# The second norm's rows turned by a VectorE block transpose and a DRAM scratch, with several groups of instructions set elsewhere

## The reference

```
h = layernorm(x)
q, k, v = h @ wq.T + bq, h @ wk.T + bk, h @ wv.T + bv        # 32 heads of 32
scores  = einsum('bshd,bstd->bsht', q, k) / sqrt(32)         # heads against heads, within one row
context = einsum('bsht,bstd->bshd', softmax(scores), v)
x = x + context
h = layernorm(x)
top-2 of 8 experts by h @ gate_w.T, softmax over the two
x = x + h @ base_w.T + base_b + 2 * (LoRA, rank 16, of the chosen experts)
```

## Time and profile before

| | us |
|---|---|
| median of 3 runs | 1341.43 (1341.17 to 1341.87) |
| the profiled execution, its time | 1342.09 |
| its span, first to last instruction | 1339.8 |
| PE busy | 1276.6 (95%) |
| DVE busy | 1113.1 (83%) |
| ACT busy | 694.4 (52%) |
| POOL busy | 274.0 (20%) |

### The profile page before, as it was taken

How to read it: one execution, slowest core, us unless ns; L and a number is a source line. 1 busy time by engine, 2 the same in 40 slices (tenths; PEclk the granted TensorE clock), 3 DMA queues, 4 the chain that set the end, 5 groups by cost and what they waited for, 6 DMA issues and landing times.

```text
span 1339.8 us, 29902 instructions
## 1 busy us (share of the span) xinstructions
PE 1276.6 (95%) x12260; PEld 669.7 (50%) x12260; DVE 1113.1 (83%) x1590; ACT 694.4 (52%) x1080; POOL 274.0 (20%) x301
## 2 busy tenths in 40 slices
PE   4766999999999999999999999999999999999996
PEld 1433555555555555555555555545555555455543
DVE  5877888888888888888888888888888888888873
ACT  6775545444555454445555544455455444554540
POOL 0021212222112122222121222222222221121120
PEclk9988999999999999999999999999999999999998
DMA  9532221233322212322222222322212233222110
GB/s 363 220 95 46 84 75 50 63 78 78 78 59 66 66 60 63 78 78 67 66 70 58 60 71 78 78 63 67 74 52 57 78 79 78 63 64 73 36 33 32
DMA packets 162008, 103.68 MB, mean 77 GB/s; under 512 B 135616, under 2 KB 136640, under 8 KB 161984
## 3 DMA queue, kind: packets, MB, share of 16 engines
q1 hardware_dynamic: 161984, 103.36, 28.0%
HBM read 69.78 MB, written 16.78 MB: 65 GB/s over the span
## 4 chain that ended last, share of the span: by engine, by line
PE 90%; DVE 4%; ACT 3%; issue 2%; DMA 0%; SPq 0%; POOL 0%; DVEq 0%; ACTq 0%; POOLq 0%
PE acc L1235 24%; PE acc L1244 24%; PE dense_acc L1351 23%; PE attn_ps L1301 7%; PE dense_acc L1359 4%; PE attn_ps L1309 2%; PE low_ps L1334 1%; PE low_ps L1336 1%; PE low_ps L1335 1%; ACT work L357 1%; PE dense_acc L1374 1%; ACT base_parts L575 1%; DVE v_parts L842 1%; DVE base_parts L842 1%; ACT w_hi_q L599 0%
## 5 line engine op out<-in xcount | busy, mean ns | idle before, releaser
L1351 PE MATMUL dense_acc<-base_parts,x 128*128 128x512 f16 x1488 | 329.8, 379 | 0.0
L357 ACT COPY work<-work 32x512 f16<-32x512 f16 x384 | 236.0, 614 | 8.6
L1351 PEld LDWEIGHTS dense_acc<-base_parts,x 128*128 128x128 f16 x1488 | 143.1, 98 | 167.0
L935 DVE SCALAR_TENSOR_TENSOR work<-acc,acc_to_a,biases_sb 128x512 f32<-128x512 f32 x192 | 143.6, 749 | 51.0 <-PE acc L1244 45.7
L1235 PE MATMUL acc<-w_hi_k,x_hi 128*128 128x512 f16 x496 | 119.2, 384 | 6.0 <-DVE x_lo L966 6.0
L1235 PE MATMUL acc<-w_hi_q,x_hi 128*128 128x512 f16 x496 | 118.8, 383 | 0.0
L1244 PE MATMUL acc<-w_hi_q,x_lo 128*128 128x512 f16 x496 | 118.3, 382 | 0.0
L1244 PE MATMUL acc<-w_hi_k,x_lo 128*128 128x512 f16 x496 | 117.7, 380 | 0.0
L1244 PE MATMUL acc<-v_parts,x_lo 128*128 128x512 f16 x496 | 117.2, 379 | 0.0
L1235 PE MATMUL acc<-v_parts,x_hi 128*128 128x512 f16 x496 | 117.2, 379 | 0.0
L527 POOL TENSOR_TENSOR work<-work 128x1024 f16<-128x1024 f32 x31 | 66.0, 2130 | 231.0 <-ACT work L732 231.0
(11 more groups left out here) (194 smaller groups left out, 2136.2 us busy)
## 6 DMA issues: line engine op xcount, KB each, us to landing
work<-x_dram SPq DMA_DIRECT2D x64, 512.0 KB, 3.7
work<-work SPq DMA_DIRECT2D x256, 64.0 KB, 2.0
work<-x_dram SPq DMA_DIRECT2D x124, 128.0 KB, 3.7
out_dram<-work SPq DMA_DIRECT2D x31, 512.0 KB, 2.9
work<-wT_dram SPq DMA_DIRECT2D x17, 512.0 KB, 5.8
v_parts<-wT_dram SPq DMA_DIRECT2D x8, 512.0 KB, 13.7
base_parts<-wT_dram SPq DMA_DIRECT2D x5, 512.0 KB, 11.3
biases_sb<-bias_dram SPq DMA_DIRECT2D x4, 512.0 KB, 8.0
```

The source lines that it names most:

```text
L357: copy(diag[c * QD:(c + 1) * QD, :, c, j::NQ, :], src).then_inc(vdiag_ready, 1)
L935: nc.vector.scalar_tensor_tensor(out=ev[:, s], in0=acc[bank][:, :], scalar=acc_to_a[:, i:i + 1], in1=bias[g][:, s], op0=ALU.mult, op1=ALU. ...
L1351: nc.tensor.matmul(dense_acc[n][:, :], rows_part[:, k, :], w_part[:, k, cols], start=(k == 0 and m == 0), stop=False)
```

## The change

The rows of the second norm are no longer turned by PE, except those of the last tile. DVE transposes `xn` in blocks of 32 x 32 into `soft` (`turn_x2`, after `norm2`). ACT issues four DMAs (`park_x2`) that write it to a DRAM scratch in the order of a full transpose, in runs of 32 floats, and one DMA (`fetch_x2`) that reads it back into `soft`. `x2_high` and `x2_low` then read `soft` instead of PSUM. They stand later: `x2_high` after q's high part, `x2_low` after v1; the subtraction L1178 waits for `x2lo_ready`.

On PE `context(t-1)` moves into k's first half, ahead of the third of the eight `x_lo` matmuls; `experts(t-1)` moves behind the scores; `spread_stats` moves ahead of q's first half. On ACT `x1_high` moves from behind the first quarter of `spread_v` to behind `x2_high`, and `gate_exp` behind the exponential; on DVE `gate_top` moves behind L1178. v's loads share the semaphores of k's.

```diff
@@ scalar
+            def park_x2(p):
+
+                act.wait_ge(x2_turned, p + 1)
+                dst = turn_dram.rearrange("(b c) (k q t) -> q c k b t", b=NQ, k=KC, q=NQ)
+                for q in range(NQ):
+                    src = x2_flat[q * QD:(q + 1) * QD, :].rearrange("c (k b t) -> c k b t", k=KC, b=NQ)
+                    act.dma_start(dst[q], src).then_inc(x2_parked, 16)
+
+            def fetch_x2(p):
+
+                act.wait_ge(x2_parked, 16 * NQ * (p + 1))
+                act.dma_start(x2_flat, turn_dram).then_inc(x2_fetched, 16)
...
                 if nxt:
                     row_statistics(t + 1)
                     normalise_quads(t + 1)
+                park_x2(t - 1)
                 act.wait_ge(at_ready, t + 1)
...
                 nc.scalar.copy(k_parts[:, 0, :, :], turned3).then_inc(a_hi_ready, 1)
-                x2_high(t - 1)
+                fetch_x2(t - 1)
                 act.wait_ge(bt_ready, t + 1)
...
                 nc.scalar.copy(dense_parts[:, :, 0, :], turned3).then_inc(b_hi_ready, 1)
+                x2_high(t - 1)
+                if nxt:
+                    x1_high(t + 1)
...
+                act.wait_ge(shifted, t + 1)
+                nc.scalar.activation(soft, soft, ACT.Exp, scale=score_undo[:, 0:1]).then_inc(exped, 1)
                 if prev:
                     gate_exp(t - 1)
-                act.wait_ge(shifted, t + 1)
-                nc.scalar.activation(soft, soft, ACT.Exp, scale=score_undo[:, 0:1]).then_inc(exped, 1)
...
                 if nxt:
-                    x1_high(t + 1)
                     low_copy(t - 1)
@@ vector
+            def turn_x2(p):
+
+                dve.wait_ge(xn2_ready, p + 1)
+                dve.wait_ge(pt_ready, p + 1)
+                nc.vector.transpose(x2_flat, xn).then_inc(x2_turned, 1)
...
                     norm2(t - 1, x1)
+                    turn_x2(t - 1)
                     turn_first(t)
...
                 add_bias(t, 1, SECOND, 0, b_acc, b_biased)
-                x2_low(t - 1)
...
                 add_bias(t, 1, "v", 2, v_acc, v_biased)
+                x2_low(t - 1)
...
-                if prev:
-                    gate_top(t - 1)
                 dve.wait_ge(scored, t + 1)
+                dve.wait_ge(x2lo_ready, t)
...
                                         ALU.subtract).then_inc(shifted, 1)
+                gate_top(t - 1)
@@ tensor
                 for k in range(KC):
+                    if k == 2 and inside is not None:
+                        inside()
                     mm = nc.tensor.matmul(dst, x_lo[:, k, :], w_hi[g][:, k, cols], start=False, stop=(k == KC - 1))
...
-                project(FIRST, 0, 0, a_acc, any_low[0])
-                context(t - 1)
+                project(FIRST, 0, 0, a_acc, any_low[0], lambda: context(t - 1))
...
-                project(SECOND, 0, 2, b_acc, any_low[0])
                 if nxt:
                     spread_stats(t + 1)
+                project(SECOND, 0, 2, b_acc, any_low[0])
...
                 project(SECOND, 1, 0, b_acc, any_low[0])
-                turn2(t - 1)
...
                 project("v", 1, 2, v_acc, any_low[0])
-                experts(t - 1)
...
                 attend(scored)
+                experts(t - 1)
```

More of the change, by code:

```diff
@@ L228, in block_kernel @@
         low_ps = ps("low_ps", [P, HALF])
-        w_loaded = {g: [sem(f"w_{g}_loaded{k}") for k in range(KC)] for g in GROUPS}
+        w_loaded = {g: [sem(f"w_{g}_loaded{k}") for k in range(KC)] for g in ("k", "q", "base")}
+        w_loaded["v"] = w_loaded["k"]
+        loads = {"k": 1, "q": 1, "v": 2, "base": 1}
         ag_loaded = sem("ag_loaded")
@@ L343, in block_kernel @@
         base_free = sem("base_free")
+        x2_turned = sem("x2_turned")
+        x2_parked = sem("x2_parked")
+        x2_fetched = sem("x2_fetched")
+        turn_dram = nc.dram_tensor("turn_dram", (P, HID), F32, kind="Internal").ap()
         block = ctx.enter_context(nc.Block())
@@ L349, in block_kernel @@
         x1_last = soft
+        x2_flat = soft
+        x2_f32 = x2_flat.rearrange("p (k n) -> p k n", k=KC)
         C_ACT_FIRST, C_ACT_LAST, C_DVE = (0, 1), (2,), (3,)
@@ L581, in sums @@
                 for k in order[g][first:last]:
-                    act.wait_ge(w_loaded[g][k], 16)
+                    act.wait_ge(w_loaded[g][k], 16 * loads[g])
                     magnitude_sum(staged[g][k], w_chunk_sum[:, j, k:k + 1])
@@ L623, in x1_high @@
                     act.wait_ge(x1_turned_ready, t)
-                    act.wait_ge(scored, t)
+                    act.wait_ge(v_acc, 2 * t)
                     nc.scalar.copy(x_hi[:, :, :], x1_turned).then_inc(xhi_ready, 1)
@@ L631, in x2_high @@
                     act.wait_ge(w_lo_done["base"], place["base"][KC - 3] + 1)
-                act.wait_ge(turned2, p + 1)
-                nc.scalar.copy(x2_hi, rows_ps).then_inc(x2hi_ready, 1)
+                if isinstance(p, int) and p == T - 1:
+                    act.wait_ge(turned2, 1)
+                    nc.scalar.copy(x2_hi, rows_ps).then_inc(x2hi_ready, 1)
+                else:
+                    act.wait_ge(x2_fetched, 16 * (p + 1))
+                    nc.scalar.copy(x2_hi, x2_f32).then_inc(x2hi_ready, 1)
+            def park_x2(p):
[7 more added lines that the diff above has]
+                act.dma_start(x2_flat, turn_dram).then_inc(x2_fetched, 16)
             x1_high(0)
@@ L970, in x2_low @@
                 dve.wait_ge(x2hi_ready, p + 1)
-                nc.vector.tensor_tensor(x2_lo, rows_ps, x2_hi, ALU.subtract).then_inc(x2lo_ready, 1)
+                src = rows_ps if isinstance(p, int) and p == T - 1 else x2_f32
+                nc.vector.tensor_tensor(x2_lo, src, x2_hi, ALU.subtract).then_inc(x2lo_ready, 1)
+            def turn_x2(p):
+                dve.wait_ge(xn2_ready, p + 1)
+                dve.wait_ge(pt_ready, p + 1)
+                nc.vector.transpose(x2_flat, xn).then_inc(x2_turned, 1)
             x1_low(0)
@@ L1049, in norm2 @@
                 else:
-                    dve.wait_ge(turned2, p)
+                    dve.wait_ge(x2_turned, p)
                 normalise(p, 1, x1, rstd_ready2, xn2_ready)
@@ L1228, in _, with project @@
             pe.wait_ge(consts_set, EXPERTS + 4)
-            def project(g, n, bank, done, any_low):
+            def project(g, n, bank, done, any_low, inside=None):
                 cols = slice(n * HALF, (n + 1) * HALF)
```

## The result

The changed kernel takes 1453.43 us (median of 4 runs, 1452.43 to 1457.04), the kernel before 1341.38 beside it: 1.084 times as long, 95% interval 1.0822 to 1.0854. That is 112 us slower; 1451 was forecast. The profiled execution, the longest of the four (1457.04), has a span of 1454.7 us, 114.9 more than before.

A forecast was written before the change was run, and what follows sets the result against it. PE was taken as the bound, with 0.8 and 0.55 us of slack ahead of its waits. 30 x (2.69 + 0.84) + 4 = 110 on 1342.1 gave 1452, as median 1451 us; range 1385 to 1545.

The forecast's parts named there:

- The order around the context: PE inside k's first half: waits 0.9 us for ACT's last quarter of `spread_v`; context runs from S + 16.7.
- The chain to the scores: From a0 to POOL's low part of q: `b_lo_ready` at S + 39.65, PE waits 2.8 us, period 41.15 against 38.46.
- The other condition of the scores: SP's eight spreading DMAs: issued by 37.4, 2.3 us before the scores; nothing added, up to 1 us.
- The issue on ACT: Four parking DMAs ahead of k's high part on ACT: 2.95 us of issue, taken from L422 on SP; bounds 1.4 and 5.
- Rivals 1 and 3: ACT's DMA issue is cheap, 0.35 each, 1396 us, chance 18%; or slow, 1.25 each, 1530 us, chance 10%.
- The landing: Parked rows in DRAM: land 3.8 us after the last issue, covered by q's transpose unless over 5.2.
- Rival 2: Parking writes to DRAM in 128 bytes land late, 7.6 us; period +2.5, clock falls each time, 1546 us; chance 17%.
- The clock: PE's granted clock falls after its wait: 1.4 us lost in six of ten steps, 0.84 a step.
- rival 1: ACT's DMA issue at 0.35 each: period 40.15, PE's wait 1.85, no clock term, 1396 us; chance 18%.
- Start and tail: Step 1, q's first half behind `spread_stats`, about 2 us; tail, tile 30's experts and later DVE, about 2; together 4.
- Rival 4: The chain to the scores hides and PE stays the bound: 1315 us; chance 5% together with rival 5, nothing changes.

The follow-up runs named there:

- a_lowcopy: The changed kernel with ACT's `low_copy` behind the second quarter of `spread_v` instead of ahead of it; 1423.48 us, ratio 1.0629.
- b_context: The kernel before with one edit, the context inside k's first half; 1366.01 us, ratio 1.018.
- b_both: The kernel before with context inside k's first half and experts behind the scores, gate steps as in the change, rows still turned by PE; 1389.35 us, ratio 1.0365.
- a_turn_small: The changed kernel with `turn_x2` turning only 32 of the 1024 columns, the rest left out; 1402.21 us, ratio 1.0459.
- a_park_sp: The changed kernel with the four parking DMAs issued by SP ahead of k's spreading, the fetch still on ACT; 1419.84 us, ratio 1.0582.
- a_floor: The changed kernel with context between k's halves, `low_copy` behind the second quarter of `spread_v` and parking issued by SP; 1361.89 us, ratio 1.0154.
- a_between: The changed kernel with the context back between k's two halves; 1417.12 us, ratio 1.056.
- a_experts_first: The changed kernel with the context between k's halves and the experts ahead of the scores; 1421.77 us, ratio 1.0618.
- b_experts: The kernel before with the experts behind the scores and the gate steps set as in the change; 1362.78 us, ratio 1.0166.
- a_busy: The changed kernel with 12 matmuls of constant weights, result unused, ahead of the wait for the scores' data; 1433.58 us, ratio 1.0692.
- a_between_busy: a_between with 8 matmuls of constant weights, product unused, ahead of the wait for the scores' data; 1387.43 us, ratio 1.035.
- a_park_double: The changed kernel with the four parking DMAs issued twice, the second time to another scratch, the fetch waiting for all eight; 1611.53 us, ratio 1.2021.

## Why the prediction was right, step by step

**The order around the context:** wait forecast 0.9, measured 0.73; context at S + 16.7, measured the same. a_lowcopy shows the cause: `low_copy` behind the second quarter removes the wait. b_context shows that the context's new place alone already runs into it.

**The chain to the scores:** `b_lo_ready` forecast at S + 39.65, measured 39.74 (730.81 less 691.07); the wait 2.8, measured 2.94; the undisturbed period 41.15, measured 41.4. Of the 2.95 us over the old 38.45, 1.55 come with the two moves alone (b_both, 40.0), 1.4 with the DRAM route. In the latter, `turn_x2` is worth 1.0 (a_turn_small) and the issue on ACT 0.9 (a_park_sp); the removal of `x2_low` from ahead of q's transpose works against them. It was not tried by itself, but the traces of b_both and of the changed kernel show it side by side. From the transpose of `attention_end` to POOL's end it is 18.12 us in b_both (602.29 to 620.41) and 19.43 here (711.38 to 730.81). `turn_first` starts 1.28 later behind `norm2`, `first_low` 1.08 later behind `turn_first`, and q's transpose 1.06 earlier behind b1 (0.78 instead of 1.84); the rest is equal. That is 1.30 of the 1.4. The forecast 1.26 for `x2_low` held a wait of 0.17 that the reordered step no longer has. The moves of `spread_stats` and `x1_high` were not tried by themselves; this comparison leaves them nothing in the steady part. The removed transposes, 0.87, are in the wait: b_both with them waits 0.69, the changed kernel 2.94, and 0.69 + 1.4 + 0.87 is 2.96.

**The other condition of the scores:** the prediction counted SP's spreading to the end of its issue, 2.3 us before the scores, and added nothing, at most 1 us. The scores wait for the landing, about 1.6 later: 0.73 us to spare, not 2.3. Adding nothing was right by that much, and a_park_sp and a_floor, which shorten the other chain or delay this one, ran into it.

**The issue on ACT:** forecast 2.95 for four, measured 2.96, with 706 ns as the median of one, so L422 on SP was the right row. Rivals 1 and 3 are out.

**The landing:** forecast 3.8, measured 3.3 for the parking, less than the 3.7 of the loads L432 in the same runs of 128 bytes. Rival 2 is out. The Trainium skill ("DMA: Bandwidth & Descriptors", Specifications) says that the DMA engine does read-modify-write below 512 bytes; in this trace the writes in such runs landed no later than the reads.

**The clock:** forecast 1.4 in six of ten steps, 0.84 a step; measured 1.53 in five of ten, 0.78. The loss at one fall came from a row and was nearly right. How often it falls was luck: I tied the fall to the length of the wait. It falls in 20 of 30 steps at 2.18 us (a_between), in none of the profiled steady part at 3.2 (a_experts_first) and in none at 1.91 (a_turn_small). So rival 1's assumption that a shorter wait has no clock term would have been a gamble.

**Start and tail:** forecast 2 and 2, measured 3.8 and -0.65. For the start the forecast had q's first half behind `spread_stats` as the cause. That is not shown: b_both leaves `spread_stats` where it was and has the scores of tile 1 at 140.4, as late as the changed kernel; a_floor has it moved, and they start at 137.9, where the kernel before has 136.9. What makes the start longer stays open.

The wrong sign of the tail is the step that failed, worth 2.65 us in all. The forecast put the experts of tile 30 ahead of a context that already waits, and counted them in full. But in that place they take up PE's wait: it was 2.54 us and is 0.62 in the changed kernel, and the context behind it takes 1.52 instead of 2.75, since the clock no longer falls there. b_experts, which has only this move, shows the same, and its tail from the scores of tile 31 on is 46.5 us, before 49.3. The context of tile 31 in the changed kernel and in b_experts:

```profile
1421.28 1.52 PE L1343 MATMUL attn_ps<-work 128*32 128x128 f16 x96 [0.62 <-ACT work L367]
...
1328.06 1.52 PE L1300 MATMUL attn_ps<-work 128*32 128x128 f16 x96 [1.19 <-ACT work L357]
```

The other parts of the change take back 2.1 of the 2.8 us.

**Rival 4,** PE stays the bound, would need the chain 1.6 us shorter. a_floor is the best that three mends give, and its mean period is 39.1, above 38.46.

## What to carry to other kernels

When the bound engine never waits, list for each of its waits by how much the data come too early: 0.8 and 0.55 us here. A move that pulls the demand forward by more than this slack costs the difference in every step, even if no engine gets any more work. By the same account, taking work away ahead of a wait gains no more than the slack; this was not tried by itself. For a DMA the slack counts to its landing, not to its issue. DMAs issued from a compute engine cost that engine's queue their whole issue time, 0.7 us each for the four in short runs and 0.36 for the plain one here, and what stands behind them in the queue must be able to bear it.

## What the runs showed of the hardware that I had not expected

The length of a wait alone does not tell whether TensorE's clock falls. Waits of equal length within one kernel (2.18 us in a_between, 2.9 in the changed kernel) were followed by scores of 1.52 us at one step and 2.75 at another. The 3.2 us waits in the steady part of a_experts_first's profile left them all at 1.52, though one of its other executions was 7 us longer at a lower mean clock. In a_floor, with waits of 1.3, the scores were slow once, behind a wait of 2.48. Filling the wait with matmuls whose result is thrown away held the clock at 1.00 and was worth 20 us (a_busy) and 30 us (a_between_busy). What decides at which steps it falls was not settled.

The second group of four DMAs on one queue, issued straight behind four others, took 3.59 us where the first took 3.03 (a_park_double; over the run the median of one is 885 ns against 706). Eight spreading DMAs right behind four parking DMAs took 5.38 us to issue instead of 5.00, and the last landed 2.12 us after it instead of 1.59 (a_park_sp).
